# Placing the small tensors last in on-chip memory, in a four-block graph network kernel

## The reference

```python
def _L0_gnn_ref(x, adj, W):
    agg = jnp.einsum('bij,bjf->bif', adj, x) / jnp.maximum(deg, EPS)
    cat = jnp.concatenate([x, agg], axis=2)
    out = jnp.einsum('bnf,of->bno', cat, W)
    return jax.nn.relu(out)
...
# L1: three times  adj @ (x @ W) + b, relu after the first two
# L2: attention, 8 heads of 64; attn = 0.33*softmax + 0.33*adj + 0.33*exp(-adj)
# L3: q, k, v; w = softmax_nodes(sum((q k^T / 8) * adj)); out = w * v
...
x = _layernorm(x + _L0_gnn_ref(x, adj, L0_gnn_W), axis=-1)
x = _layernorm(x + _L1_gnn_ref(...), axis=-1)
x = _layernorm(x + _L2_gnn_ref(...), axis=-1)
x = _layernorm(x + _L3_gnn_ref(...), axis=-1)
```

## The kernel before

| step | moving | stationary | matmuls |
|---|---|---|---|
| adjacency products (aggregate, hidden twice, gcn_out) | sup or adjT, 256 | adjT or sup | 48 |
| queries and keys (`qk`) | x2T, 256 | wqkv | 48 |
| output projection (`project_out`) | wout, 256 | oT | 24 |
| second and third support | w123, 256 | hidT | 24 |
| first support, block 0's support0 and self_product | w123, w0, 256 | fT | 36 |
| values | wqkv, 512 | x2T | 12 |
| last block's projection | w3, 384 | x3T | 12 |
| scores (line 1107; 64 partitions each, issued in pairs) | qkT, 256 | qkT | 48 = 24 pairs |
| attend (line 1134), float32 | work, 256 | v_sb | 16 (32 in the trace) |
| transposes (line 932), float32 | ident, 128 | x, work | 44 |

## Time and profile before

### The profile page before, as it was taken

How to read it: one execution, slowest core, us unless ns; L and a number is a source line. 1 busy time by engine, 2 the same in 40 slices (tenths; PEclk the granted TensorE clock), 3 DMA queues, 4 the chain that set the end, 5 groups by cost and what they waited for, 6 DMA issues and landing times.

```text
span 1322.8 us, 30265 instructions
## 1 busy us (share of the span) xinstructions
PE 1296.0 (98%) x11036; PEld 1190.9 (90%) x11036; DVE 1204.9 (91%) x3820; ACT 914.4 (69%) x2444; POOL 138.6 (10%) x265
## 2 busy tenths in 40 slices
PE   7899999999999999999999999999999999999995
PEld 7799999999999999999999999999999998999984
DVE  4798999999999999999999999999999999999995
ACT  4576776776776776776776776776676776676672
POOL 0000011011111011111011111011111011111011
PEclk9999999999999999999999999999999999999998
DMA  5111111001111001111001111101111101110000
GB/s 189 34 34 35 34 42 42 25 19 42 42 42 42 25 19 42 42 43 42 27 17 42 42 42 43 29 15 43 42 42 42 32 12 42 42 42 9 9 10 24
DMA packets 51314, 49.00 MB, mean 37 GB/s; under 512 B 7904, under 2 KB 50656, under 8 KB 51168
## 3 DMA queue, kind: packets, MB, share of 16 engines
q1 hardware_dynamic: 51168, 47.08, 11.6%
HBM read 38.68 MB, written 8.39 MB: 36 GB/s over the span
## 4 chain that ended last, share of the span: by engine, by line
PE 95%; DVE 2%; ACT 1%; DMA 0%; issue 0%; SPq 0%; POOL 0%; POOLq 0%; DVEq 0%
PE psum L918 63%; PE psum L932 12%; PE psum L1134 9%; PE psum L1107 8%; PE psum L1187 1%; PE psum L1190 1%; PE psum L1199 1%; DMA w_raw<-in_L_gnn_W 0%; PE psum L1209 0%; DVE bn L571 0%; DVE wqkv_l L555 0%; DVE x L608 0%; ACT wqkv_h L321 0%; POOL rstd L306 0%; ACT qkv L321 0%
## 5 line engine op out<-in xcount | busy, mean ns | idle before, releaser
L454 ACT ACTIVATE work<-work,shift 128x256 f32<-128x256 f32 x512 | 254.8, 500 | 33.8 <-DVE shift L744 33.8
L763 DVE SCALAR_TENSOR_TENSOR work<-work,rsum,extra 128x256 f32<-128x256 f32 x512 | 217.0, 475 | 0.2
L321 ACT ACTIVATE work<-psum 128x512 f32<-128x512 f32 x256 | 138.3, 596 | 76.4 <-PE psum L932 72.2
L744 DVE CUSTOM_DVE_ANT_0 work<-psum,minus_big 128x256 f32<-128x256 f32 x512 | 189.8, 417 | 1.3 <-PE psum L1107 1.2
L321 ACT ACTIVATE sup_h<-psum 128x512 fp32r<-128x512 f32 x128 | 75.9, 593 | 161.2 <-PE psum L918 161.2
L303 POOL TENSOR_TENSOR mv<-mv,eps 128x2 f32<-128x2 f32 x128 | 32.2, 252 | 1170.0 <-DVE mv L592 1170.0
L918 PE MATMUL psum<-x2T_h,wqkv_h 128*128 128x256 f32 x512 | 144.9, 283 | 0.0
L918 PE MATMUL psum<-x2T_h,wqkv_l 128*128 128x256 f32 x512 | 142.2, 278 | 0.0
L918 PE MATMUL psum<-x2T_l,wqkv_h 128*128 128x256 f32 x512 | 142.2, 278 | 0.0
L932 PE MATMUL psum<-ident,work 128*128 128x128 f32 x1024 | 129.4, 275 | 0.0
L1134 PE MATMUL psum<-work,v_sb 128*64 128x256 f32 x1024 | 124.7, 385 | 0.0
(11 more groups left out here) (134 smaller groups left out, 3778.7 us busy)
## 6 DMA issues: line engine op xcount, KB each, us to landing
xT_sb<-in_xT SPq DMA_DIRECT2D x32, 256.0 KB, 2.8
adjT_sb<-in_adjT SPq DMA_DIRECT2D x32, 256.0 KB, 3.2
adj_sb<-in_adj SPq DMA_DIRECT2D x32, 256.0 KB, 4.8
x_sb<-in_x SPq DMA_DIRECT2D x32, 256.0 KB, 4.9
out<-y_sb SPq DMA_DIRECT2D x32, 256.0 KB, 4.4
work<-in_L_gnn_W_qkv SPq DMA_DIRECT2D x1, 1536.0 KB, 8.4
mask_row<-in_nodemask SPq DMA_DIRECT2D x32, 32.0 KB, 4.6
w_raw<-in_L_gnn_W SPq DMA_DIRECT2D x3, 256.0 KB, 5.3
```

The costliest lines, as they stand in the source:

```text
L321: return nc.scalar.activation(dst, src, ACT.Copy, scale=scale)
L454: last = nc.scalar.activation(prob[:, p % 2, i, h], prob[:, p % 2, i, h], ACT.Exp, bias=shift[:, p % 2, h, i:i + 1], scale=-1.0, accum_out ...
L744: last = V_.tensor_tensor_reduce(out=prob[:, p % 2, i, h], in0=bank(SCORES[p] + h)[:, i * N:(i + 1) * N], in1=minus_big[:, g % 2, i], scal ...
L763: last = V_.scalar_tensor_tensor(out=prob[:, p % 2, i, h], in0=prob[:, p % 2, i, h], scalar=rsum[:, p % 2, h, i:i + 1], in1=extra[:, g % 2 ...
```

## The change

The declarations of 20 small tensors, each under 1 KB on a partition (`b1_col`, `b2_col`, `one`, `minus_half`, `eps`, the masks but `mask_all`, `deg`, `rdeg`, `shift`, `psum_exp`, `rsum`, `gate`, `gate_max`, `gate_shift`, `gate_sum`, `gate_rsum`, `gate_col`), are moved behind the last large one, ahead of `bn`, `mv` and `rstd`. No tensor changes its size. A function `load_nodes` is added among SyncE's, and nothing calls it.

No instruction is added, removed or moved: on every engine the instructions of the kernel after stand in the same order, with the same shapes and waits, and only their line numbers (8 higher behind the declarations) and their operands' addresses differ.

```diff
-        b1_col = sb("b1_col", [P, FT])
-        b2_col = sb("b2_col", [P, FT])
         b3_row = sb("b3_row", [P, F])
         bout_row = sb("bout_row", [P, F])
         ident = sb("ident", [P, P])
-        one = sb("one", [1, 1])
-        minus_half = sb("minus_half", [P, NT])
-        eps = sb("eps", [P, NT])
...
-        mask_all_u8 = sb("mask_all_u8", [G, N], nodemask.dtype)
         mask_all = sb("mask_all", [G, N])
-        mask_col = sb("mask_col", [P, NT, G])
-        big_col = sb("big_col", [P, NT, G])
-        mask_row = sb("mask_row", [P, 2, N], nodemask.dtype)
...
         adj_junk = sb("adj_junk", [P, NT, N])
-        deg = sb("deg", [P, NT])
-        rdeg = sb("rdeg", [P, NT])
         extra = sb("extra", [P, 2, NT, N])
...
-        shift = sb("shift", [P, 2, 2, NT])
-        psum_exp = sb("psum_exp", [P, 2, 2, NT])
-        rsum = sb("rsum", [P, 2, 2, NT])
...
         y_sb = sb("y_sb", [P, 2, NT, F])
         wout_raw = y_sb.rearrange("p b t f -> p (b t) f")
+        b1_col = sb("b1_col", [P, FT])
+        b2_col = sb("b2_col", [P, FT])
+        one = sb("one", [1, 1])
...
+        gate_col = sb("gate_col", [P, NT])
         bn = sb("bn", [P, 4, NT, 6])
...
+            def load_nodes(g):
+                fetch(adj_sb, adj_d, g, dma_adj)
+                fetch(x_sb, x_d, g, dma_x)
...
```

More of the change, by code:

```diff
@@ L117, in graph_blocks_kernel @@
         gate_junk = sb("gate_junk", [P, NT, 2, D])
+        gate_exp = sb("gate_exp", [1, N])
+        gate_prob = sb("gate_prob", [1, N])
+        x4_pre = sb("x4_pre", [P, NT, F])
+        y_sb = sb("y_sb", [P, 2, NT, F])
+        wout_raw = y_sb.rearrange("p b t f -> p (b t) f")
+        b1_col = sb("b1_col", [P, FT])
+        b2_col = sb("b2_col", [P, FT])
+        one = sb("one", [1, 1])
+        minus_half = sb("minus_half", [P, NT])
+        eps = sb("eps", [P, NT])
+        mask_all_u8 = sb("mask_all_u8", [G, N], nodemask.dtype)
+        mask_col = sb("mask_col", [P, NT, G])
+        big_col = sb("big_col", [P, NT, G])
+        mask_row = sb("mask_row", [P, 2, N], nodemask.dtype)
+        deg = sb("deg", [P, NT])
+        rdeg = sb("rdeg", [P, NT])
+        shift = sb("shift", [P, 2, 2, NT])
+        psum_exp = sb("psum_exp", [P, 2, 2, NT])
+        rsum = sb("rsum", [P, 2, 2, NT])
         gate = sb("gate", [P, NT])
@@ L122, in graph_blocks_kernel @@
         gate_rsum = sb("gate_rsum", [1, 1])
-        gate_exp = sb("gate_exp", [1, N])
-        gate_prob = sb("gate_prob", [1, N])
         gate_col = sb("gate_col", [P, NT])
-        x4_pre = sb("x4_pre", [P, NT, F])
-        y_sb = sb("y_sb", [P, 2, NT, F])
-        wout_raw = y_sb.rearrange("p b t f -> p (b t) f")
         bn = sb("bn", [P, 4, NT, 6])
@@ L236, in load_x @@
                 fetch(xT_sb, xT_d, g, dma_xT)
+            def load_nodes(g):
+                fetch(adj_sb, adj_d, g, dma_adj)
+                fetch(x_sb, x_d, g, dma_x)
+                sp.dma_start(mask_row[:, g % 2], nodemask[bass.ds(g, 1)].broadcast_to([P, N])) \
+                    .then_inc(dma_mask_row[g % 2], 16)
             def load_rest(g):
```

## The result

The kernel after takes 1339.3 us (median of four runs, 1338.16 to 1341.05) where the kernel before, on the same chip, takes 1323.6 us (1322.3 to 1326.87): a ratio of 1.0116, with a 95% interval of 1.0092 to 1.014. The predicted 1288 us was wrong in its direction. The time is that of the slower rival, which had given 1340 us. Times of whole kernels are medians of 4 to 25 executions each, which lie within 0.4% of one another but for one of ten in experiment 5 (minus), 4467.7 us, which is left out.

What follows compares the result with a forecast made beforehand. PE's matmul distances were taken to bound the kernel, 32 turns of 39.65 us plus some 54 us of filling and draining. 1324.6 - 43 (denser products) + 6.4 (new waits) = 1288 us; range 1268 to 1340.

Steps and rivals of the forecast that it cites:

- slower rival: PE's matmuls: operands that begin alike hinder each other, 113 ns products go to 120; 15.6 us more, 1340 us; chance 0.24.
- What bounds the kernel: Steady middle: PE's matmul distances are the time, 39.65 us a turn; DVE, busy 37.27 us, has 2.4 us to spare.
- Part (a): PE's matmuls: moving and stationary operands at remainder 0 stand denser, 1.35 us a turn less, 43 us over 32 turns.
- The 6.4 us: PE and DVE, both nearly full: new waits on one another, 0.2 us a turn, added back to the forecast.
- What was set against it: project_out: wout by oT stands 32 apart and is at 120 ns too, held against operands that begin alike being the slow ones.
- The same remainders at 113 and 119: Two qk steps, x2T by wqkv: equal remainders give 113 and 119 ns, so something beside the start decides too.
- case of no change: PE's matmuls: the excess may belong to float32r itself, whatever the address, so time stays 1324.8 us; chance 0.26.
- the first case: Float32r products on PE get denser: faster, likeliest 1288 us, own range 1266 to 1303; chance 0.50.
- (b): DVE, ACT and POOL work: durations change by -0.5% to +2%, hidden by PE; taken as zero.
- (c): Transfers: destinations shift by 32 or 96 bytes modulo 128; 2.8 us to landing, issued a turn ahead, hidden; zero.
- (d): The added function: called by nobody, order of instructions the same on every engine; zero.
- The floor of 109 to 113 ns: Under PE's matmul distances: each product also needs a weight load of 128 columns; 256-column products taken at 112 ns.

Runs made afterwards that it cites:

- experiment 5: Kernel after, with pads putting the stationary operand 64 bytes (plus) or 192 bytes (minus) beyond the moving one modulo 256 in most products: 1324.6 and 1326.8 us.
- experiment 1: Kernel after with one 32-byte pad ahead of the first tensor, so all large tensors begin at remainder 32 modulo 128: 1339.0 us, ratio to before 1.0097.
- experiment 2: Kernel after with pads putting fT, sup, hidT, x2T, oT, x3T at remainder 64, weights and adjT at 0: 1316.8 us, ratio to before 0.993.
- experiment 4: Separate kernels: TensorE alone, stretches of 48 float32r matmuls at 28 sets of starts and columns; then with ACT and DVE working beside: spans 232.0 and 232.8 us.
- experiment 3: Kernel after with activations at 32, weights and adjT at 0: 1331.1 us; with activations at 96, weights and adjT at 32: 1317.6 us.
- experiment 9: Separate kernel, TensorE alone: operands 0 to 112 bytes apart in steps of 16, six entries each; 64 apart gave 113.3 to 117.8 ns.
- experiment 8: Separate kernel, TensorE alone: stretches of 48 matmuls 64 apart, entered behind varying transposes or 12 other matmuls: 113.3 or 117.8 ns at the same addresses.
- 7: Kernel before with two pads moving sup alone from remainder 96 to 32, adjT staying at 96: 1323.1 us, ratio to before 0.9983.
- 6: Kernel after with activations 64 bytes apart from weights and adjT, plus qkT_l moved 64 bytes from qkT_h: 1314.9 us, ratio to before 0.9918.

## Why the prediction was wrong

**What bounds the kernel: right.** PE's distances were the time, before and after: PE's busy time and the span grew by 13.4 and 13.6 us, and DVE kept its 37.3 us a turn.

**Part (a), the price of remainder 0: the step that failed.** It took 112 ns for 256 columns, 221 for 512 and 168 for 384, and 113 for a pair of scores; measured were 119 to 120, 231, 177 and 119 to 120. Its sum, 1.35 us a turn less, came out as 0.43 us a turn more. The reading beneath it, that an operand off a boundary pays for further pieces of 64 bytes, finds no support in experiment 1, where no operand is on the boundary and nothing changes, and is refuted by experiment 2, where the activations go from one boundary of 64 bytes to the next, which by this reading costs and gains nothing, and the time falls by 22 us. That 6.6 and 13.3 ns are 16 and 32 columns was taken for evidence. It was two numbers that fitted a story, and no row at remainder 0 stood behind it. What decides in its place is how the two operands of a matmul begin relative to one another: all alike 1339 us, 32 apart 1331, 64 apart 1315 to 1327. The 6.4 us that the sum gave back for waits of PE and DVE on one another were not put to the test, since PE's turn grew.

**The slower rival: right, in mechanism and nearly in size.** Its sign came, hidT from 113 to 120 ns. It had 15.6 us; the medians differ by 15.7, which is luck to that digit, and the spans by 13.6. Its terms: qk 32 x 24 x (6.7 + 1.5) = 6.3 us against 5.9 measured, hidT 5.1 against 4.2, fT 4.1 against 3.6 + 0.6. It lacked 1.2 us of small losses and the 1.9 us that 512 and 384 columns gain by beginning alike (experiment 4 shows such gains alone). What was set against it, wout by oT 32 apart at 120, was no counterexample: 32 apart is little better than alike (117 to 120 in experiment 3, 118.2 to 118.3 in experiment 9). That it is the two streams of reads that get in each other's way is its picture of the cause; the runs show the dependence on the starts, and not what happens inside.

**The same remainders at 113 and 119: noted, and not used.** The prediction held it for the case of no change. It fits the two levels: experiment 8 gives both at the same addresses, by the entry alone. For w0 by fT the prediction took 118 (support0) and 113 (self_product), a mean of 115.5; the trace has 115.4.

**The case of no change: wrong, and so is what it drew from the cache lines.** By the prediction's use of the 16-byte cache lines on the Trainium skill's page "SBUF — State Buffer", section "SBUF: two separate sides", every kernel here would take one time. The runs have 24 us between them. And the Trainium skill's page "TensorE: Matmul & The Clock Gate", section "Step-by-step: what each phase is for", says that loading the next weights takes nothing from the running matmul, since each has a read port of its own. The runs do not bear that out for float32r: the starts of the two streams, and at 64 apart the entry, move 256-column matmuls between 113.3 and 120.0 ns, with no other engine at work. The prediction's "the transposes agree (108)" is a slip: the 109.2 ns that it takes from the Trainium skill are for 256 columns, and a transpose here has 128, for which that rule would give 128/2.4 + 2.5 = 55.8 ns against 109 measured. Only the 1262 us at the far end of the first case leaned on the rule.

**Parts (b), (c), (d), each taken at zero: right.** 594, 403 and 2.7 against 596, 403 and 2.8; instructions and their order are the same. Part (b) had read y_sb's 396 ns as the mark of remainder 0; x keeps 403 at remainder 0, so it is not. **The floor of 109 to 113 ns under 256 columns: right as far as seen.** No stretch of TensorE alone was below 113.3, and matmuls of 128 columns stood at 111.7; that the weight loads set this was not tested. **Transposes** stayed at 109 to 110, whatever the remainders.

**Open.** What exactly the two streams share. Half of 128 bytes being the best and 0 and 112 the worst would fit a memory that repeats every 128 bytes and serves one of the two at a time, but no run shows that inside, and 128 apart (118.7) and both at 16 (118.3) do not fit it. How the entry picks the level was shown in its effect, not in its cause, so that experiments 5 and 7 cannot be worked out ahead. Of five kernels with 64 apart, three gained 0.7 to 0.8% on the kernel before (experiments 2, 3 and 6) and two gained nothing (experiment 5), so each placement has to be measured, and again after any change of the order of stages.

## What to carry to other kernels

Where PE bounds a kernel of float32r products, look at how the moving and the stationary operand begin relative to one another, modulo 128 bytes. Placed alike they cost 120 ns for 256 columns here, 64 apart 113 to 118; so "align everything" can be the worst arrangement, and a pad of 64 bytes in front of the activations is a cheap thing to measure. Against all alike it gave 0.9 to 1.8%, but which of the two levels a stage falls into could not be told ahead. When a prediction rests on a value that has no row (here remainder 0), a pattern without exception among the rows that are there (here: no equal starts below 120) deserves the larger chance.

## What the runs showed of the hardware

- Float32r matmuls of 256 columns back to back, by relative start modulo 128: 119.7 to 120.0 ns alike (118.3 with both at 16), 118.2 to 118.3 at 32, 113.3 or 117.8 at 64, 119.8 to 120.3 at 112. A common offset of 32 bytes changes nothing, in a whole kernel (1339.0 and 1339.3 us; 1317.6 and 1316.8) or alone; 128 apart is at 118.7, not quite like 0.
- At 64 apart there are two steady levels, 113.3 and 117.8 ns. At the same addresses what ran ahead picks one (in one kernel 5 transposes instead of 6 were enough; in another 5 gave the other level), and a stretch of 48 keeps it.
- Longer matmuls turn it round: 512 columns stand at 227.1 to 227.2 ns alike and 233.3 at 64 apart, 384 columns at 173.3 to 173.7 and 173.3 to 176.7.
- ACT and DVE at work beside 20 of 28 stretches left these distances as they were, but for one stretch (16 apart, 118.3 for 120.0).
